# A landing wait ahead of each gather of GpSimd, with the gathers counted on two semaphores by even and odd

## What is computed

```
xp = x @ w_in + b_in
h = gelu(batchnorm(depthwise3x3(x)))
offset = (h @ w_off + b_off).reshape(N, H, W, G, P, 2)
mask = softmax((h @ w_msk + b_msk).reshape(N, H, W, G, P))
y = dcn_core(xp, offset, mask) @ w_out + b_out      # bilinear sampling
x = x + gamma1 * layer_norm(y)
x = x + gamma2 * layer_norm(gelu(x @ w_fc1) @ w_fc2)
```

## Time and profile before

| What | Value |
|---|---|
| Median of the three executions | 8874.52 us |
| Span of the profiled execution | 14589.8 us |
| PE busy in it | 5727.1 us, 39% |
| DVE busy | 5562.0 us, 38% |
| ACT busy | 3113.0 us, 21% |
| POOL busy | 6510.0 us, 45% |
| Mean share of full TensorE clock | 0.662 |

### The profile page before, as it was taken

One profiled execution on the slowest core, in us unless ns is written; L12 is line 12 of the kernel. 1 busy time (PEld: TensorE's weight loads), 2 busy tenths in 40 slices (PEclk: granted clock), 3 DMA queues, 4 the chain that ended last, 5 costly groups with the idle time before them and its releaser, 6 DMA issues.

```text
span 14589.8 us, 92590 instructions
## 1 busy us (share of the span) xinstructions
PE 5727.1 (39%) x24752; PEld 3652.5 (25%) x24752; DVE 5562.0 (38%) x11869; ACT 3113.0 (21%) x7121; POOL 6510.0 (45%) x6898
## 2 busy tenths in 40 slices
PE   3334344343433434334343333433435343442336
PEld 1112222222322223122232222312223222221224
DVE  3334334343343433434334343343433443333334
ACT  1112222222211222122221212212222121221123
POOL 5454444444444443454434444354443445445431
PEclk6666667666666667666666666766667666665667
DMA  4221112121121211212112121121211221111110
GB/s 72 50 48 39 45 41 44 45 45 43 39 45 43 44 43 36 50 43 45 41 38 46 42 46 41 37 51 42 47 41 36 49 42 48 37 38 45 43 35 13
DMA packets 851934, 626.11 MB, mean 43 GB/s; under 512 B 551018, under 2 KB 734562, under 8 KB 851472
## 3 DMA queue, kind: packets, MB, share of 16 engines
q0 software_dynamic: 221200, 452.62, 11.5%
q1 hardware_dynamic: 629600, 167.72, 7.3%
q10 hardware_dynamic: 672, 0.24, 0.0%
HBM read 549.46 MB, written 70.57 MB: 42 GB/s over the span
## 4 chain that ended last, share of the span: by engine, by line
another core or an unknown queue 33%; PE 24%; issue 23%; DVE 14%; ACT 5%; DMA 1%; SPq 0%; DVEq 0%; ACTq 0%
PE bank L1542 4%; PE bank L1508 3%; PE bank L1682 3%; PE bank L1594 3%; PE bank L1659 2%; PE bank L1432 2%; DVE y L1047 2%; PE bank L1517 2%; PE bank L1472 1%; ACT arena L838 1%; DVE ring L1037 1%; ACT xflat L789 1%; DVE nwt L955 1%; DVE cmax L1156 1%
## 5 line engine op out<-in xcount | busy, mean ns | idle before, releaser
L708 POOL DMA_INDIRECT ring<-column_table,idx_r x6860 | 6486.4, 946 | 7804.9 <-DMA wts_r<-corner_weight 5723.4
L1542 PE MATMUL bank<-v,pT 112*112 112x128 f32 x6496 | 995.9, 305 | 1865.8 <-issue 952.5
L1047 DVE TENSOR_REDUCE y<-ring 128x128 f32<-128x4608 f32 (+1 forms) x196 | 1572.3, 8022 | 16.8 <-remote 12.0
L1542 PEld LDWEIGHTS bank<-v,pT 112*112 112x112 f32 x6496 | 916.3, 202 | 2144.6 <-issue 1156.1
L1489 PE MATMUL bank<-ident,xn 112*128 112x112 f32 x224 | 55.3, 402 | 3369.7 <-remote 1866.9
L1508 PE MATMUL bank<-kT,qT 128*112 128x448 f32 (+3 forms) x1792 | 933.8, 618 | 786.2 <-issue 463.7
L1037 DVE TENSOR_TENSOR ring<-ring,bank 128x4608 f32<-128x4608 f32 (+1 forms) x196 | 970.0, 4949 | 120.8 <-remote 78.4
L1156 DVE TENSOR_REDUCE cmax<-arena 112x1 f32<-112x448 f32 (+3 forms) x896 | 504.4, 574 | 1121.7 <-ACT arena L820 709.6
L1489 PEld LDWEIGHTS bank<-ident,xn 112*128 112x128 f32 x224 | 37.1, 217 | 3379.5 <-issue 2511.2
L1517 PE MATMUL bank<-ident,arena 112*112 112x112 f32 x3248 | 547.6, 294 | 769.3 <-ACT arena L838 548.3
L802 ACT ACTIVATE xnT<-bank 128x448 f32<-128x448 f32 x56 | 30.4, 543 | 3628.1 <-issue 2168.4
(11 more groups left out here) (176 smaller groups left out, 8202.5 us busy)
## 6 DMA issues: line engine op xcount, KB each, us to landing
ring<-column_table,idx_r POOLq DMA_INDIRECT x6860
xflat<-dense_rows SPq DMA_DIRECT2D x56, 406.0 KB
column_table<-proj SPq DMA_DIRECT2D x196, 112.0 KB
corner_weight<-wts_s SPq DMA_DIRECT2D x56, 252.0 KB
wts_r<-corner_weight SPq DMA_DIRECT2D x196, 72.0 KB
hT<-dense_rows SPq DMA_DIRECT2D x224, 56.0 KB
tin<-tokens SPq DMA_DIRECT2D x56, 224.0 KB
out<-xn SPq DMA_DIRECT2D x56, 224.0 KB
```

What stands on the lines that cost most here:

```text
L708: pool.indirect_dma_start(ring[:, r, e * CORNERS:(e + 1) * CORNERS, :].rearrange("p s c -> p (s c)"), None, source, bass.IndirectOffsetOnA ...
L1047: dve.tensor_reduce(y[:, k % BLK % 2].rearrange("p (g c) -> p g c", g=G), ring[:, bass.ds(t % RING, 1)].rearrange("p o (g e) c -> p (o g) ...
L1542: ins = pe.matmul(bank[1][0:TT, 0:C], pT[:, c % 2, t], v[:, NT * c + t], start=(c == 0 and t == 0), stop=(c == j and t == nt - 1))
```

## The change

GpSimd waits ahead of gather e of a tile (from e = 2) for the landing of gather e-2 of the same tile. To have a count that says this exactly, each slot gets two semaphores: even gathers (18 of the 35) count on `gathered[0][r]`, odd ones (17) on `gathered[1][r]`. A wait for the last but one then asks for all gathers of that parity so far. The first two gathers of a tile have no such wait. The wait for a whole tile (`tile_landed`) asks both semaphores. Each wait is followed by an increment of a semaphore that nobody reads (`pool_passed`). One constant, `w_out4`, is loaded on the second semaphore of the last slot so that both of its semaphores start at 16.

```
+OF_PARITY = ((FETCHED + 1) // 2, FETCHED // 2)
...
-        gathered = [sem(f"gathered{i}") for i in range(RING)]
+        gathered = [[sem(f"gathered{parity}_{i}") for i in range(RING)] for parity in range(2)]
...
-                const(w_out4[:, :], w["w_out4"])
+                pool.dma_start(w_out4[:, :], w["w_out4"]).then_inc(gathered[1][RING - 1], 16)
...
                     for e in range(FETCHED):
+                        if e > 1:
+                            two_before_landed(q, r, e)
                         pool.indirect_dma_start(
                             ring[:, r, e * CORNERS:(e + 1) * CORNERS, :].rearrange("p s c -> p (s c)"), None,
                             source, bass.IndirectOffsetOnAxis(ap=idx_r[:, r, e:e + 1], axis=0),
-                        ).then_inc(gathered[r], 16)
+                        ).then_inc(gathered[e % 2][r], 16)
                         if e == 5:
-                            if r:
-                                pool.wait_ge(gathered[r - 1], q * (16 * FETCHED) + 16 * FETCHED)
-                            else:
-                                pool.wait_ge(gathered[RING - 1], q * (16 * FETCHED) + PRIMED)
-                            pool.sem_inc(tile_ready, 1)
+                            tile_landed(q, r - 1)
+
+            def two_before_landed(q, r, e):
+                pool.wait_ge(gathered[e % 2][r], q * (16 * OF_PARITY[e % 2]) + 16 * (e // 2) + (PRIMED if r == RING - 1 else 0))
+                pool.sem_inc(pool_passed, 1)
+
+            def tile_landed(q, r):
+                for parity in range(2):
+                    whole = 16 * OF_PARITY[parity]
+                    pool.wait_ge(gathered[parity][r], q * whole + (whole if r >= 0 else PRIMED))
+                    pool.sem_inc(pool_passed, 1)
+                pool.sem_inc(tile_ready, 1)
```

More of the change, by code:

```diff
@@ L231, in build @@
         passed = sem("passed")
+        pool_passed = sem("pool_passed")
         table_zeroed = sem("table_zeroed")
@@ L674, in _ @@
             pool.wait_ge(zeroed, 1)
-            pool.dma_start(gidx[:, :], consts["gidx"]).then_inc(gathered[RING - 1], 16)
+            pool.dma_start(gidx[:, :], consts["gidx"]).then_inc(gathered[0][RING - 1], 16)
             zero_borders(pool, 0, border_out)
@@ L725, in _ @@
                     fill_ring(q, table[0:(n + 1) * POS * G * PAD])
-            pool.wait_ge(gathered[RING - 1], 16 * FETCHED * (TILES // RING) + PRIMED)
-            pool.sem_inc(tile_ready, 1)
+            tile_landed(TILES // RING, -1)
         @block.scalar
@@ L998, in shift_grid @@
                 dve.wait_ge(b_om_in, 16)
-                for x_ in (iw_out[0], iw_out[1], gathered[RING - 1]):
+                for x_ in (iw_out[0], iw_out[1], gathered[0][RING - 1]):
                     dve.wait_ge(x_, PRIMED)
@@ L1009, in late_constants @@
                 dve.wait_ge(cst_in, 16 * NCONST[0])
-                for x_ in (tok_out[0], tok_out[1], o_out):
+                for x_ in (tok_out[0], tok_out[1], o_out, gathered[1][RING - 1]):
                     dve.wait_ge(x_, PRIMED)
```

## The result

The changed kernel takes 12,589.6 us (median of four, 12,584.7 to 12,598.2) against 8872.7 us before: a ratio of 1.419, interval 1.417 to 1.421. The forecast was 11,650 us with a range from 10,200 to 12,100. The direction and the mechanism were right, the size was not: 42% slower in place of 31%.

A forecast was written before the change was run, and what follows sets the result against it. POOL, gathering without a stop, was taken as the bound. 196 tiles of 58.4 us (17 x 3.36 + 1.25) give 11,440 us; with 52 us ahead and 153 us behind, 11,645 us; range 10,200 to 12,100 us.

The forecast's parts named there:

- The bound of the runs: POOL gathers without a stop, starts 1.25 us apart, 8574 us in all; the other engines need about 8430 us.
- The quiet pair: Two gathers on POOL: 2.48 us from start to seen landing plus 0.80 us of hand-over, 3.28 us.
- the first rival: POOL's hand-over is mostly hidden: a pair takes 2.88 us, the program 10,050 us, half hidden about 10,850; chance 0.13.
- The second rival: The wait is met anyway: a pair needs 2.50 us or less, the program stays at 8874 us; chance 0.05.
- The term for traffic: Gather landings that meet the other queue's transfers (7.3% of DMA time) come 1.1 us later: 0.08 us a pair.
- theory L: Experiments' theory: gather starts at the later of previous start + 1.249 us and awaited landing + 0.771 us; late landings are traffic.
- The extra instructions and the wait for the whole tile: Some 33 semaphore instructions per tile on POOL, and the wait behind the sixth gather: nothing counted; instructions uncovered 110 us.
- The ends: 52 us ahead of the first gather and 153 us behind the last one.
- The other engines' slack: DVE, ACT, PE and SP's loads need about 8430 us and now have 11,440, so they are always ready.
- later landings: Rival: a third of gather landings take 3.6 us, a pair 3.65 us, the program 12,600 us; chance 0.07 over 12,100.
- A bound of 15,100 us: Upper bound if every gather landing takes 3.6 us: 4.4 us a pair, 76.1 us a tile.
- The third rival of the prediction: Faster: gathers held apart give DVE's dependent steps room, about 8700 us; chance 0.03.

The follow-up runs named there:

- the contiguous store: Changed kernel with the store of dense rows as 112 pieces of 96 bytes in place of 2688 single floats: 12,148 us on chip A, 12,140 us on another.

## Why the prediction was right in kind and wrong in size

**The bound of the runs: right, for a partly wrong reason.** The prediction took the interval of 1.25 us from a trace that was 1.64 times too long, and held POOL for the bound. A trace of before of the right length confirms it. It is the page's group of the gathers and what POOL waited for:

```profile
span 8880.5 us, 92590 instructions
...
POOL 52%; issue 21%; PE 13%; DVE 7%; DMA 4%; ACT 2%; SPq 1%; POOLq 0%; DVEq 0%; ACTq 0%; another core or an unknown queue 0%
...
L708 POOL DMA_INDIRECT ring<-column_table,idx_r x6860 | 6528.4, 952 | 2150.1 <-issue 2066.1
```

```profile
L708 POOL DMA_INDIRECT ring<-column_table,idx_r x6860: 938/944/1449, 52.0 to 8702.0; - x196
its engine sat idle before it (us, times) until:
  issue: 2066.1, 6779
  DMA ring<-column_table,idx_r: 54.0, 72
  DMA wts_r<-corner_weight: 30.1, 9
```

The gathers take 8702.0 - 52.0 = 8650 us, 76 more than 6859 x 1.25, and 178 us follow the last one (153 were counted). The wrong part is the cause of the long trace. The prediction spoke of what holds "outside the profiler". The profiler is not the cause, since 8880.5 us were measured with it too, and on chip A all twelve executions take some 14,478 us. That the long trace came from a chip like A is inferred from its length and from the held-up steps told of below; which chip it was isn't on record.

**The quiet pair: right.** 2.48 + 0.80 = 3.28 us were forecast. The timeline after has 3.22 to 3.34, and over all 6468 waits the median is 2.54 us from a gather's start to the passing of its wait and 0.771 us from there to the next start. That the hand-over isn't hidden behind gather e-1 was right as well, so the first rival falls. The second rival, that the wait is met anyway, falls too: counted from the pass of one wait to the pass of the wait for that gather, a quiet gather takes 3.3 us here. The Trainium skill (DMA: Bandwidth & Descriptors, "Anatomy of one DMA") has about 2.0 us plus bytes over 436 GB/s, an estimate of 2.15 us for the 64 KB here; the measurement decides.

**The term for traffic: the step that failed.** The prediction added 0.08 us to a pair, 267 us in all: 7.3% of the DMA time times 1.1 us for a landing that meets it. In the trace after, 642 of the 6468 waits (10%) pass more than 3 us behind their gather's start, and on average 2.6 us later than a quiet one; 101 of them pass more than 9 us behind it, and each of these 101 gathers starts within 12 us of one of the 56 stores. The share was a fair number, the price of an encounter was not. The chain of theory L, replayed with this trace's landings, gives from first to last gather 12,187 us, and 11,286 us if all were quiet: late landings cost 902 us, 0.27 us a pair, 3.4 times the term. 407 to 450 us of that are the store of single floats. The rest is spread over transfers of which none was tried by itself.

The 1.1 us came from a single wait of the earlier trace rows, and the trace at hand could hardly show more: POOL's queue had passed late landings without looking, and at 52 of the 56 stores POOL started no gather in the 10 us that followed, since it stood there waiting. In the trace of 8880.5 us it started 6 to 8 gathers behind each.

**The extra instructions and the wait for the whole tile: nearly right.** Nothing was counted for either. The instructions cost nothing as such, as the run with twelve under way shows, and the wait for a tile holds nobody: gather 6, behind it, follows gather 4 by the quiet 3.30 us. But the lead had hidden two pauses of GpSimd's own. Gather 7 of a tile (counted from 0) starts 1.69 us after its wait has passed (median), where the others take 0.77 to 0.78, and gather 8 takes 0.95. The kernel with one gather under way has such a pause as well, at gather 8. And in 41 of the 48 later passes of the loop the first gather comes some 2.1 us late. By the same replay the first costs 110 us and the second 88. What GpSimd does in them stays open.

**The sum.** From first to last gather the prediction had 11,440 us and the trace after has 12,386. The difference of 946 us is, by the replay, 112 us for the quiet pair (3.31 in place of 3.28), 635 for the late landings beyond their 267, and 198 for the two pauses. The ends came out 6 us shorter than counted.

**The other engines' slack: right.** DVE stands waiting for the tile's `tile_ready` for 4744.0 us in the trace after, against 824.5 in the trace of before of 8880.5 us, so the others have more room than they had (who waited for whom: us in total, times, longest):

```profile
DVE ring L1047 <- POOLq L730: 4744.0, 168, 49.4
```

```profile
DVE ring L1037 <- POOLq L719: 824.5, 75, 24.7
```

**The range.** It gave later landings 0.07, above 12,100 us, with 12,600 us as their price. The time is almost that number, but by luck: the rival had a third of the landings at 3.6 us because pairs further apart meet more loads. Measured, a tenth is later than 3 us, a few of them by far more than 1.1 us, and the bursts were there before. A bound of 15,100 us stood in the text, and the range should have reached further toward it, since the term came from one row.

## What to carry to other kernels

When a wait for a DMA's landing is put in the issuing queue, count the time from one hand-over to the next (here 2.5 us to see the landing and 0.8 us to start the next gather) against what is under way times the issue interval; three gathers were enough to hide the quiet case, four did not hide the worst, and twelve did.

A queue that runs ahead hides late landings as well as it hides waits, so a trace made with it doesn't show their price. Look for stretches where the DMA engines are full at few GB/s, and in these for stores of single elements; here one such store of 10.5 KB, made 56 times, was near half of it. Small pauses of the issuing queue itself come out of hiding in the same way.

When the span of a trace and the times of runs differ by more than a few per cent, settle whether they come from like chips before any wait of the trace is used; intervals on the bounding engine survived here, sums of waits did not.

## What the runs showed of the hardware that was not expected

**One program, two times.** On chip A the kernel before takes 14,478 us, on two others 8875 to 8877 us. The difference is not in how long DVE's operations take: it is busy 5562.0 us in the earlier trace rows and 5588.5 us in the trace of 8880.5 us. PE is busy 5727.1 us in the one and 5317.2 in the other, at a mean granted clock of 0.662 and 0.775 of full speed; these 410 us are small beside the 5700 by which the spans differ. A part of it is in when dependent steps start; how large a part was not worked out. The waits of one such pair of small operations on DVE (who waited for whom: us in total, times, longest), on chip A with three gathers under way, with four, and with twelve:

```profile
DVE nwt L971 <- DVE nwt L969: 36.0, 39, 1.2
```

```profile
DVE nwt L971 <- DVE nwt L969: 189.2, 172, 1.2
```

```profile
DVE nwt L971 <- DVE nwt L969: 236.9, 207, 1.3
```

The pair is executed 675 times. The trace ahead of the prediction has 191 such waits and 196.0 us for the same pair. In the changed kernel, in its variant on chip A with the contiguous store, and in the trace of before of 8880.5 us there is no such wait: the second operation starts 34 ns after the first ends. A held-up step starts 0.9 to 1.1 us late on average (the sums above over their counts), a little less than an interval of gathers. On chip A it happens the more often the more gathers are queued: to 39, 172 and 207 of the 675 pairs, of which some 320 fall between running gathers in each of the three traces. With two under way it happened to none, there in the variant only. On the other chips it happens with no number.

**What the change is worth then depends on the chip.** With the contiguous store the changed kernel takes 12,148 us on chip A and 12,140 us on another. Landings, POOL and "issue" make up 98% of the chain that ended last in both places. The kernel is 0.839 of before on the one and 1.369 of before on the other. By adding the 407 to 450 us of the store, the changed kernel itself would take 12,550 to 12,600 us on chip A, 0.87 of before; that is an estimate. The third rival of the prediction, room for the other engines, so has a true core on chip A, and none where the forecast was to be met. Why dependent steps are held up there stays open: no experiment here changes anything on the chip's side, and chip A was seen in one set of executions only, so a passing condition of that chip can't be told from the chip itself.
